# Block attention on one core: the stationary values of PV widened from 9 to 32 columns per head

## What is computed

```
q = (x @ Wq.T + bq).reshape(B, S, 16, 8)      # k and v in the same way
scores = einsum('bihd,bjhd->bhij', q, k) / sqrt(8)
allowed = blk[:, None] >= blk[None, :]        # blk = position // 32
scores = where(allowed, scores, 0)            # masked scores are 0, not -inf
probs = softmax(scores)
ctx = einsum('bhij,bjhd->bihd', probs, v).reshape(B, S, 128)
x = x + ctx @ Wo.T + bo
```

## Time and profile before

| | |
|---|---|
| runs | 1664.58, 1664.86, 1678.32 us; median 1664.86 |
| profiled execution, its time | 1668.52 us |
| profiled execution, span of its instructions | 1666.5 us |
| mean granted TensorE clock | 0.845 of 2.4 GHz |
| busy: PE, PEld, DVE, ACT, POOL | 88%, 58%, 50%, 54%, 17% |
| preparation of block attention (after its layer norm) | 1168.8 to 1220 us of the span |
| main loop of block attention | 1221.9 to 1626 us |

### The profile page before, as it was taken

How to read it: one execution, slowest core, us unless ns; L and a number is a source line. 1 busy time by engine, 2 the same in 40 slices (tenths; PEclk the granted TensorE clock), 3 DMA queues, 4 the chain that set the end, 5 groups by cost and what they waited for, 6 DMA issues and landing times. The chain is left out here.

```text
span 1666.5 us, 26411 instructions
## 1 busy us (share of the span) xinstructions
PE 1471.6 (88%) x9399; PEld 959.6 (58%) x9400; DVE 833.4 (50%) x1461; ACT 900.2 (54%) x1582; POOL 281.1 (17%) x206
## 2 busy tenths in 40 slices
PE   3599999999999999999999982691889999999995
PEld 2376667666666766766666662461555555555443
DVE  5355445445544554455455443353685555554506
ACT  2267667666767767677677651230534444444443
POOL 3233123113312321231133112103100000000000
PEclk9799999999999999999999995795865557665557
DMA  4442244234234423433342335112000000000001
GB/s 139 110 108 73 66 105 107 51 97 108 69 76 105 106 55 80 107 90 71 90 107 69 76 95 177 43 47 57 1 1 1 1 1 1 1 1 1 1 1 31
DMA packets 53495, 105.22 MB, mean 63 GB/s; under 512 B 9010, under 2 KB 30004, under 8 KB 53300
## 3 DMA queue, kind: packets, MB, share of 16 engines
q1 hardware_dynamic: 52004, 100.59, 24.4%
q0 software_dynamic: 1424, 3.67, 0.8%
HBM read 18.70 MB, written 5.31 MB: 14 GB/s over the span
## 5 line engine op out<-in xcount | busy, mean ns | idle before, releaser
L505 DVE TENSOR_REDUCE a_negmax<-a_score 128x1 f32<-128x1024 f32 x257 | 314.8, 1225 | 406.5 <-PE a_score L371 406.5
L466 ACT ACTIVATE a_probs_T<-a_tr 128x512 f32<-128x512 f32 x514 | 279.2, 594 | 256.2 <-PE a_tr L377 256.2
L472 ACT ACTIVATE a_probs<-a_score,a_negmax 128x1024 f32<-128x1024 f32 x256 | 286.4, 1119 | 28.7 <-DVE a_negmax L505 28.6
L430 PE MATMUL a_out<-a_probs_T,a_v 128*64 128x256 f32 x2088 | 283.0, 392 | 0.6 <-DVE a_attn_T L521 0.6
L377 PE MATMUL a_tr<-ident,a_probs 128*128 128x128 f32 x2056 | 267.4, 273 | 0.0
L377 PEld LDWEIGHTS a_tr<-ident,a_probs 128*128 128x128 f32 x2056 | 240.7, 140 | 35.5 <-issue 0.6
L1298 DVE TENSOR_REDUCE a_lowest<-a_score 128x1 f32<-128x512 f32 (+3 forms) x320 | 183.7, 631 | 129.0 <-PE a_score L1174 76.6
L1266 ACT ACTIVATE a_probs_T<-a_score_T 128x1024 f32<-128x1024 f32 (+1 forms) x192 | 149.2, 810 | 168.0 <-PE a_score_T L1154 149.6
L430 PEld LDWEIGHTS a_out<-a_probs_T,a_v 128*64 128x64 f32 x2088 | 126.8, 136 | 116.5 <-issue 66.9
L1171 PE MATMUL a_score<-a_k_all,a_q_all 32*128 32x512 f32 (+3 forms) x384 | 162.4, 599 | 6.6 <-DVE a_lowest L1298 6.4
L331 POOL TENSOR_TENSOR a_rden<-a_rden_col,a_ones 128x256 f32<-128x256 f32 x65 | 68.4, 1052 | 574.8 <-DVE a_rden_col L528 574.8
(11 more groups left out here) (235 smaller groups left out, 2161.5 us busy)
## 6 DMA issues: line engine op xcount, KB each, us to landing
a_q_rot<-a_q_raw SPq DMA_DIRECT2D x68, 128.0 KB, 2.3
a_k_rot<-a_k_raw SPq DMA_DIRECT2D x68, 128.0 KB, 2.3
a_xn_cur<-normed_T SPq DMA_DIRECT2D x17, 512.0 KB, 3.2
a_k_stack0ah<-a_k_hi SPq DMA_DIRECT2D x18, 256.0 KB, 3.3
a_k_stack0al<-a_k_lo SPq DMA_DIRECT2D x18, 256.0 KB, 4.7
a_k_stack0bh<-a_k_hi SPq DMA_DIRECT2D x18, 256.0 KB, 5.0
a_k_stack0bl<-a_k_lo SPq DMA_DIRECT2D x18, 256.0 KB, 4.7
a_k_stack1ah<-a_k_hi SPq DMA_DIRECT2D x16, 256.0 KB, 3.3
```

Of the source, the lines that this page charges most:

```text
L430: ins = nc.tensor.matmul(out_ps[64 * h:64 * h + 64, 0:256], v[par if s >= 5 else 1 - par][:, k, 64 * h:64 * h + 64], probs_T[grp][:, h, k, ...
L466: nc.scalar.activation(probs_T[(s - 1) // 4 % 2][:, h, 4 * i:4 * i + 4, tile % 2 * P:tile % 2 * P + P], tr_ps[i][:].rearrange("p (k q) -> ...
L472: nc.scalar.activation(probs[s % 4][:], score_ps[s % 2][:], ACT.Exp, bias=negmax[:, s:s + 1], accum_out=den[:, s:s + 1]).then_inc(probs_re ...
L505: nc.vector.tensor_reduce(negmax[:, s:s + 1], score_ps[s % 2][:], axis=AX.X, op=ALU.max, negate=True)\
```

## The change

`v_den` gets 32 columns per head in place of 9. POOL first fills all of it with zeros and, after its wait for `zeroed`, writes the ones column. `values` takes all 32 columns as stationary operand and writes 32 partitions of `out_ps` per head. Columns 9 to 31 are zeros, so nothing else in the result changes.

```
-        v_den = sb("v_den", [P, B, TB, H1, DH1 + 1])
+        v_den = sb("v_den", [P, B, TB, H1, 32])
...
                     nc.gpsimd.memset(ones[:], 1.0)
-                    nc.gpsimd.memset(v_den[:, :, :, :, DH1:], 1.0)
+                    nc.gpsimd.memset(v_den[:], 0.0)
                     nc.gpsimd.memset(suffix[:], 0.0)
...
                     nc.gpsimd.memset(b_col[:], 0.0).then_inc(zeroed, 1)
                     pool.wait_ge(zeroed, 1)
+                    nc.gpsimd.memset(v_den[:, :, :, :, DH1:DH1 + 1], 1.0)
                     pool.wait_ge(fixed_loaded, 16)
...
                     for h in range(HG):
-                        ins = nc.tensor.matmul(out_ps[32 * h:32 * h + DH1 + 1, lo - 512 * half:512], v_den[:, b, kt, g * HG + h, :],
+                        ins = nc.tensor.matmul(out_ps[32 * h:32 * h + 32, lo - 512 * half:512], v_den[:, b, kt, g * HG + h, :],
                                                probs_T[n % 3][:, h, 0:hi - lo], start=kt == 0, stop=kt == (3, 7)[half], skip_group_check=True)
```

## The result

The changed kernel takes 1675.59 us, the median of nine runs (1671.82 to 1683.94), beside 1664.58 us for the kernel before in the same session. The ratio is 1.0092, with a 95% interval of 1.0061 to 1.0124: slower, and by the ratio within the 1% that was called no change, though the interval reaches past it. The forecast was 1673.3 us. The profiled execution took 1671.82 us, with a span of 1669.8; that is 3.3 us above the span before, though the preparation is 6.7 us longer and the main loop 4.5, because the layers ahead took 7.6 us less in this execution.

The account below looks back on a forecast made before the run. PE was taken to bound the main loop at the low clock, and POOL the preparation. Fill 6.26 us plus loads 2.1 us made 8.4 us on 1664.86, so 1673.3 us; range 1660 to 1690.

Parts of the forecast that it names:

- The fill: Preparation ahead of the main loop: POOL's zero fill of `v_den` takes 6818 ns in place of 556, so `b_col` comes 6.26 us later.
- paid in full: Preparation: PE's bias matmuls wait for POOL's `b_col` and nothing else is there for PE, so all 6.26 us count.
- The loads: PV weight loads in `values`: 23 more columns cost 22 ns per call, four heads' loads side by side, 96 calls, 2.1 us.
- The stride: Wider stride of `v_den` in the sums of later values and DVE's write: nothing, at the far end 5.1 us.
- The clock: Main loop: PE's mean granted clock stays as before, near 0.57; forecast with both terms paid has chance 0.64.
- Rival A: Main loop: fuller PV columns bring the high clock, 1572 us, about 1623 if half the loop gets it; chance 0.11.
- Rival B: Main loop: high-clock stretches are lost, up to 24 us, 1697 us with all lost, 1685 with half; chance 0.13.
- The sum: Whole kernel: fill and loads, 6.26 + 2.1 = 8.4 us, added to the median of 1664.86 us.

Follow-up runs that it names:

- e2: The kernel before with 9 columns, plus a fill of 8192 elements per partition of a scratch tile where the change fills `v_den`, ones behind `b_col`: ratio 1.0042.
- e5: The change with the fill of `b_col` moved ahead of the zero fill of `v_den`, DVE's write of the values waiting for the fills: ratio 1.0103.
- e3: The kernel before with `v_den` 32 columns wide per head in memory, only the ones filled and PV taking 9 columns: ratio 0.9945.
- e1: The change without the zero fill of all `v_den` ahead of `b_col`; ones and 23 zero columns are filled behind it: ratio 1.0021 against before.
- e4: The change without the zero fill; columns 8 to 31 per head filled with ones behind `b_col`, the added result rows unread: ratio 1.0012 against before.
- e6: The change with its zero fill of `v_den` moved into the layer norm that runs ahead: ratio 1.0051 against before.
- e10: The kernel before with the fill of `b_col` first and all fills but ones and `b_col` waiting until DVE's copies are done: ratio 1.0022.

## Why the prediction was right

**The fill, 6.26 us: right in size and place.** The slope of the fills gave 6.82 us for 8192 elements; it took 6.92, and PE's start came 6.39 us later. The step "paid in full" held, and e2 has the same start with the fill alone. Its reason was incomplete. POOL's queue was one of two paths: in the changed kernel DVE's last copy ends at 1171.64, 0.66 us before `b_col` (1172.20 + 0.10), and e5 shows that it is late for the same fills. The prediction took DVE's input as done 0.19 us early and independent of POOL, so its sum had the right term by the path that it knew of; e5, the cure by order alone, gives back 0.71 us of the start.

**The loads, 2.1 us: right in kind, too small.** The interpolation gave 22 ns for 23 columns; the row says 41 (134 less 93), since the means don't lie on one straight line: 93, 134 and 207 ns at 9, 32 and 128 columns. By the Trainium skill's page TensorE: Matmul & The Clock Gate, section LDWEIGHTS (loading the stationary operand), the difference is an estimated 19 ns, which is further off. Of a call the rows show 1.87 less 1.83, 0.04 us, or 3.8 us for 96 calls at the low clock; it is the same with 512 and with 128 moving columns, so it belongs to the load or the way out of the array and not to the stream, and no run tells these two apart. The fit over ten loops shows 2.6, give or take 0.5. The loads ran side by side as forecast, since one after another they would have cost 96 x 4 x 41 ns = 15.7 us.

**The stride, nothing:** right in its two rows (e3: 277 and 684 ns).

**The clock, unchanged:** right. With 21 runs of the change and 87 of before, the mean clock is 0.8416 beside 0.8434, a distance of 0.0018 (give or take 0.0008). The added 6.4 + 2.6 = 9.0 us at the low clock explain 9.0 x 0.0002 = 0.0018 of it, which is the whole distance. Rival A (fuller columns bring the high clock) fell with that, and with e1 and e4. Rival B (the high stretches are lost) did not come in the change either. It is a real possibility for this kernel all the same: e5, with the same columns and nearly the same start, has a mean clock 0.0070 lower than before. And single runs move by what B was priced at: loops of these twelve profiles held from 24 to 55 us at 2.4 GHz, which is 15 us of time, and e2 shows that 34 us can come with 9 columns too. In the changed kernel, a rise of the clock came after this much PV (windows of line 1189 alone):

```profile
1253.80:1257.20 3.40, 1.76 (x8) 0.03 (x4) 0.50 0.00 0
1257.20:1260.60 3.40, 0.85 (x8) 0.16 (x8) 0.99 0.00 0
1267.50:1270.90 3.40, 1.93 (x8) 0.23 (x8) 0.50 0.00 0
...
1414.30:1417.70 3.40, 1.93 (x8) 0.23 (x8) 0.50 0.00 0
```

With all 128 columns in use, 1.76 us of PV stood before a rise and 1.93 us twice before none; before the change 2.62 us of 9-column matmuls stood before two rises. The width of the stationary operand is not what decides here.

**The sum.** 8.4 us were forecast; start and loop of the profiles give 6.4 + 2.6 = 9.0, the line 10.3 and 10.7 (give or take 1.2), the means 13.4 and 9.0. The line's 1.5 us more than the profiles' sum is about the size of its error; if something else is in it, it was not found. That the change stays within 1% is shown more safely by the second session (1.0027 to 1.0082) than by the first, whose interval reaches 1.0124.

## What to carry to other kernels

Padding a stationary operand gained nothing here: the heads ran side by side with 9 columns as with 32, and the wider loads and the zero fill had to be paid. A large fill cost 6.4 us ahead of `b_col`, 2.3 us in the layer norm (e6) and nothing that shows behind `b_col` (e1, e4); ask which DVE instructions run beside it, not only who waits for its semaphore. Where single runs swing with the granted clock, compare start and loop in the profiles, or the runs at an equal mean clock; the raw ratio of one session was 1.0092 and of the next 1.0055 for the same kernel.

## What the runs showed of the hardware that was not expected

Fills on POOL hold some DVE instructions up. DVE's float32 copy of 128 x 512 took 0.43 us with no fill beside it (e10) and 7.05 us where it began within a fill of 6.92 us that another of 1.79 us followed (the change); it ended 0.28 us after the second. A TENSOR_SCALAR of 128 x 16 took 2.49 us in place of 0.17; the layer norm's statistics (e6), an addition of two tiles and short instructions on a PSUM tile (e1) were not slowed. The time saved for each us at 2.4 GHz in a loop where PE is the bound was 0.494 us, from ten profiles; if all of the loop ran twice as fast there it would be 1 us, so by this arithmetic about half of each such stretch hangs on something else; what that is no run here shows.
